# The last layer of a gated four-layer block on one core: a router moved into the attention, five shared blocks moved behind the routed tiles

## The reference, cut to what matters

```
x = x + tanh(g_xattn[3]) * attention(layernorm(x), ctx, ctx)     # 32 query heads of 8, 8 key/value heads
h = layernorm(x)
logits = h @ W_router.T                                          # 8 experts
probs  = softmax(logits);  weight, expert = top_k(probs, 2)
shared = (silu(h @ Wg) * (h @ Wu)) @ Ws_down                     # hidden width 704
shared = shared * sigmoid(h @ W_sgate.T)
sparse = sum over the two experts of weight * (silu(h @ We_g) * (h @ We_u)) @ We_down   # hidden width 176
x = x + tanh(g_ffn[3]) * (shared + sparse)
```

## Time and profile before

| | |
|---|---|
| median of 3 runs (lowest to highest) | 818.59 us (817.67 to 820.45) |
| span of the profiled execution | 816.7 us |
| PE, DVE, ACT, POOL busy | 707.3, 539.1, 353.9, 214.8 us |
| mean granted clock of PE | 0.945 |
| the fourth attention's last matmul ends | about 676 us |
| routed tiles on PE | 735.3 to 795.6 us |
| last work of DVE ends | 814.1 us |

### The profile page before, as it was taken

How to read it: one execution, slowest core, us unless ns; L and a number is a source line. 1 busy time by engine, 2 the same in 40 slices (tenths; PEclk the granted TensorE clock), 3 DMA queues, 4 the chain that set the end, 5 groups by cost and what they waited for, 6 DMA issues and landing times. The chain is left out here.

```text
span 816.7 us, 14003 instructions
## 1 busy us (share of the span) xinstructions
PE 707.3 (87%) x4479; PEld 467.5 (57%) x4485; DVE 539.1 (66%) x1627; ACT 353.9 (43%) x622; POOL 214.8 (26%) x307
## 2 busy tenths in 40 slices
PE   9999997988987785798868988986888899999995
PEld 4644466666764674576746767652233227776773
DVE  5786898788773879678861571657876756423554
ACT  2663455455445664221124314334488693212220
POOL 0002595002000132013313550632252220242340
PEclk9999999999998999789998999997599999999998
DMA  6994421040000310000160150011000043032315
GB/s 197 342 218 102 145 75 46 4 156 1 3 2 0 104 53 1 1 1 26 40 214 33 54 192 14 34 40 66 2 2 2 3 150 65 33 110 79 105 61 171
DMA packets 55566, 60.24 MB, mean 74 GB/s; under 512 B 13847, under 2 KB 48808, under 8 KB 55496
## 3 DMA queue, kind: packets, MB, share of 16 engines
q1 hardware_dynamic: 50408, 46.02, 19.6%
q0 software_dynamic: 4848, 13.28, 4.7%
q10 hardware_dynamic: 240, 0.05, 0.0%
HBM read 34.92 MB, written 24.20 MB: 72 GB/s over the span
## 5 line engine op out<-in xcount | busy, mean ns | idle before, releaser
L1928 ACT ACTIVATE arenas<-psum 128x512 f32<-128x512 f32 (+6 forms) x89 | 63.2, 732 | 60.3 <-PE psum L1134 51.6
L3156 DVE TENSOR_REDUCE arenas<-psum 128x2 f32<-128x512 f32 x96 | 62.0, 685 | 19.6 <-PE psum L1706 18.5
L943 POOL TENSOR_SCALAR arenas<-arenas,small 128x1024 f32<-128x1024 f32 x8 | 9.0, 1128 | 161.2 <-DVE small L2895 161.2
L960 POOL DMA_INDIRECT experts_l<-shared,small x30 | 29.1, 969 | 81.4 <-ACT shared L2228 72.8
L1123 PE MATMUL psum<-conb 128*128 128x512 bf16 x167 | 44.6, 413 | 4.9 <-ACT early L1928 3.1
L1134 PE MATMUL psum<-conb,shared 128*128 128x128 bf16 (+2 forms) x512 | 39.2, 231 | 10.3 <-issue 5.7
L1134 PE MATMUL psum<-con,early 128*128 128x128 f32 (+1 forms) x188 | 33.3, 287 | 15.5 <-ACT late L1928 4.4
L1134 PEld LDWEIGHTS psum<-conb,shared 128*128 128x128 bf16 (+2 forms) x512 | 34.0, 118 | 17.8 <-issue 14.9
L3121 DVE TENSOR_TENSOR shared<-shared,psum 128x128 f32<-128x128 f32 x30 | 8.6, 287 | 53.3 <-PE psum L1659 26.6
L1928 ACT ACTIVATE late<-psum 128x512 f32<-128x512 f32 (+1 forms) x51 | 25.6, 501 | 40.3 <-PE psum L1134 40.3
L2275 ACT ACTIVATE early<-psum 128x1024 f32<-128x1024 f32 x32 | 32.4, 1037 | 22.3 <-PE psum L1723 22.0
(11 more groups left out here) (436 smaller groups left out, 1792.2 us busy)
## 6 DMA issues: line engine op xcount, KB each, us to landing
sorted_l<-late SPq DMA_DIRECT2D x3, 1920.0 KB, 16.7
early<-sorted_l SPq DMA_DIRECT2D x6, 645.0 KB, 5.7
early<-in_L_ffn_sw SPq DMA_DIRECT2D x3, 1024.0 KB, 9.2
late<-sorted_l SPq DMA_DIRECT2D x23, 129.0 KB, 2.1
sorted_l<-late SPq DMA_DIRECT2D x1, 2944.0 KB, 23.5
early<-in_L_ffn_We_gate_up SPq DMA_DIRECT2D x2, 1408.0 KB
early<-in_L_ffn_expert_w SPq DMA_DIRECT2D x2, 1024.0 KB, 6.6
early<-in_L_ffn_w SPq DMA_DIRECT2D x1, 2048.0 KB, 8.2
```

Source lines behind the costliest of these rows:

```text
L960: pool.indirect_dma_start(expert_rows2[p], bass.IndirectOffsetOnAxis(dest2[p][:, i:i + 1], 0), out_r2[k], None).then_inc(outs_sent[k], 16)
L1928: act.activation(dst, view(v), ACT.Copy, scale=scale).then_inc(f.drained(i, key), 1)
L3156: dve.tensor_reduce(nm, q3d(f.slot(0, ("max", w, k)), 2, S), X, ALU.max, negate=True)\
```

## The change

The lines of the changed program are numbered by up to 29 more than those of the profile.
- The turns of batches 0 and 1 go into slot 59 of the attention, their logits into slot 62. DVE, not ACT, moves the turned rows. ACT takes the first pair's exponentials before it copies the last unit's result.
- Batch 2 is normalised alone between `results3(6)` and `results3(7)`, behind `gates3(0)`; batch 3 alone behind `results3(7)`. The turns of 2 and 3 and their logits stand between blocks of batch 0. The keys of banks 4 and 5 go in the order xT 2, gate 2, xT 3, gate 3.
- The rank stands behind the first block of batch 1.
- The half block of pair 1 stands before down product 1. The five full blocks of batch 3 follow the routed tiles: one each after steps 23 and 24 of the tile loop (its last step is 25), then two, down product 2, one, down product 3.
- DVE takes four of these blocks, adds batch 0's routed rows, adds down product 2, takes the fifth block, adds the routed rows of 1, 2 and 3, and down product 3 last.

```
@@ -648,14 +648,15 @@
...
-        plan("l3f", 0, A=([4, 5], 1, [(key, n) for p in range(2) for key in ("xT", "gate") for n in (2 * p, 2 * p + 1)]
-                          + [("dn", 0), ("dn", 1)]),
-             B=([0, 1, 2, 3], 1, [("sh", n, j) for n in range(B) for j in blocks3(n)]))
+        plan("l3f", 0, A=([4, 5], 1, [("xT", 0), ("xT", 1), ("gate", 0), ("gate", 1), ("xT", 2), ("gate", 2),
+                                      ("xT", 3), ("gate", 3), ("dn", 0), ("dn", 1)]),
+             B=([0, 1, 2, 3], 1, [("sh", n, j) for n in range(B - 1) for j in blocks3(n)] + [("sh", B - 1, SC3 - 1)]))
         plan("l3k", 0, A=([6], 1, [("rank",)]))
         tiles = range(TILES)
         plan("l3r", 0, X=([0, 1], 1, [("xT", i) for i in tiles]), U=([2, 3], 1, [("up", i) for i in tiles]),
              H=([4, 5], 1, [("hT", i) for i in tiles]), D=([6, 7], 1, [("dn", i) for i in tiles]))
-        plan("l3f", 1, A=([4, 5], 1, [("dn", 2), ("dn", 3)]))
+        BEHIND = range(SC3 - 1)
+        plan("l3f", 1, A=([4, 5], 1, [("dn", 2), ("dn", 3)]), B=([0, 1, 2, 3], 1, [("sh", B - 1, j) for j in BEHIND]))
...
+                routing = {59: [(row_turned3, 0), (row_turned3, 1)], 62: [(logits3, 0), (logits3, 1)]}
...
+                    for part, n in routing.get(g, ()):
+                        part(n)
...
-                last = ("sh", n | 1, SC3 - 1)
-                pe.wait_ge(fb.drained(0, last), fb.read(0, last))
+                last = ("sh", n | 1, BEHIND[-1] if n == B - 1 else SC3 - 1)
+                part = int(n == B - 1)
+                pe.wait_ge(fb.drained(part, last), fb.read(part, last))
...
+            def row_turned3(n):
+                p, s = n // 2, n % 2
+                pe.wait_ge(xn_ready["l3f"].sem, xn_ready["l3f"].count(n))
+                turn(pl["l3f"]["A"], 0, ("xT", n), [(P, c * S + t * P, rows3[p][:, s * T + t, c * P:(c + 1) * P])
+                                                    for c in range(DC) for t in range(T)], ident)
+
+            def logits3(n):
+                logits(pl["l3f"]["A"], 0, n, xnT3, r3T, E + 1)
+
+            def routed3(behind):
...
+                    if step >= TILES:
+                        next(behind, None)
...
-            banks_free("l3f", 0)
-            rows_turned3(0)
             tokens3(UNITS - 1)
-            for n in range(2):
-                logits(pl["l3f"]["A"], 0, n, xnT3, r3T, E + 1)
+            row_turned3(2)
             pe.wait_ge(ld["l3s"], 16 * 4)
-            shared3(0, blocks3(0))
-            rows_turned3(1)
-            for n in range(2, 4):
-                logits(pl["l3f"]["A"], 0, n, xnT3, r3T, E + 1)
-            shared3(1, blocks3(1))
+            shared3(0, 0, blocks3(0)[0:2])
+            logits3(2)
+            row_turned3(3)
+            shared3(0, 0, blocks3(0)[2:3])
+            logits3(3)
+            shared3(0, 0, blocks3(0)[3:])
+            shared3(0, 1, blocks3(1)[0:1])
             banks_free("l3k", 0)
             pe.wait_ge(picks_ready, TURNS)
             rank(pl["l3k"]["A"], 0, 2 * B, picked)
-            shared3(2, blocks3(2)[0:2])
+            shared3(0, 1, blocks3(1)[1:])
+            shared3(0, 2, blocks3(2)[0:2])
             shared_down3(0, 0)
-            shared3(2, blocks3(2)[2:])
+            shared3(0, 2, blocks3(2)[2:])
+            shared3(0, 3, [SC3 - 1])
             shared_down3(0, 1)
-            shared3(3, blocks3(3))
-            routed3()
-            banks_free("l3f", 1)
-            for n in range(2, 4):
-                shared_down3(1, n)
+
+            def behind_routed3():
+                for j in BEHIND[0:2]:
+                    shared3(1, 3, [j])
+                    yield
+                yield
+                shared3(1, 3, BEHIND[2:4])
+                shared_down3(1, 2)
+                shared3(1, 3, BEHIND[4:])
+                shared_down3(1, 3)
+
+            behind = behind_routed3()
+            routed3(behind)
+            alone(behind)
...
+                probabilities3(0)
                 sums3(UNITS - 1)
...
-            rows_moved3(0)
-            probabilities3(0)
-            shared3(0, 0)
-            rows_moved3(1)
+            row_moved3(2)
+            shared3(0, 0, blocks3(0)[0:2])
+            row_moved3(3)
+            shared3(0, 0, blocks3(0)[2:])
             probabilities3(1)
-            shared3(0, 1)
-            for n in range(2, 4):
-                shared3(0, n)
+            for n in range(1, 3):
+                shared3(0, n, blocks3(n))
+            shared3(0, 3, [SC3 - 1])
             routed3()
+            shared3(1, 3, BEHIND)
...
                 dve.wait_ge(x3_ready.sem, x3_ready.count(3))
                 norm_rows("l3f", 0, rows3[0])
                 reciprocals3(ON_POOL - 1)
+                f = pl["l3f"]["A"]
+                for n in range(2):
+                    dve.wait_ge(f.filled, f.full(0, ("xT", n)))
+                    dve.tensor_copy(xnT3[n], f.slot(0, ("xT", n))[:, 0:W]).then_inc(f.drained(0, ("xT", n)), 1)
                 results3(UNITS - 2)
+                gates3(0)
+                dve.wait_ge(x3_ready.sem, x3_ready.count(ON_POOL - 1))
+                alone(norm_steps("l3f", [2], [rows3[1][:, t, 0:D] for t in range(T)]))
                 results3(UNITS - 1)
+                alone(norm_steps("l3f", [3], [rows3[1][:, T + t, 0:D] for t in range(T)]))
...
-            gates3(0)
-            norm_rows("l3f", 1, rows3[1])
...
-            hidden3(0, 0, first_steps)
+            route3(0)
+            choices_of_pair(0)
+            hidden3(0, 0, blocks3(0)[0:1])
             gates3(1)
-            hidden3(0, 1, second_steps)
+            hidden3(0, 0, blocks3(0)[1:2])
+            route3(1)
+            choices_of_pair(1)
+            hidden3(0, 0, blocks3(0)[2:])
             alone(places(pl["l3k"]["A"], 0, places3, chosen, index_ready))
-            hidden3(0, 2, lambda j: add_shared(0, 0) if j == 1 else None)
+            hidden3(0, 1, blocks3(1))
+            hidden3(0, 2, blocks3(2)[0:2])
+            add_shared(0, 0)
+            hidden3(0, 2, blocks3(2)[2:])
+            hidden3(0, 3, [SC3 - 1])
             add_shared(0, 1)
-            hidden3(0, 3, lambda j: None)
             routed3()
-            add_shared(1, 2)
-            for n in range(B):
+            def added(n):
+                add_routed(n)
                 if n == B - 1:
                     add_shared(1, n)
-                add_routed(n)
                 dve.drain().then_inc(x_done.sem, 1)
+
+            hidden3(1, 3, BEHIND[0:4])
+            added(0)
+            add_shared(1, 2)
+            hidden3(1, 3, BEHIND[4:])
+            for n in range(1, B):
+                added(n)
```

More of the change, by code:

```diff
@@ L1807, in attention3, with shared3 @@
                         tokens3(w - 1)
+                    for part, n in routing.get(g, ()):
+                        part(n)
                 values3(UNITS - 1, 3)
-            def shared3(n, blocks):
+            def shared3(i, n, blocks):
                 f = pl["l3f"]["B"]
@@ L1813, in shared3 @@
                     if j < SC3 - 1:
-                        shared_up(f, 0, n, j, xnT3, P, j * P, H_S3 + j * P, ws_gu, ws_gu, 2 * H_S3)
+                        shared_up(f, i, n, j, xnT3, P, j * P, H_S3 + j * P, ws_gu, ws_gu, 2 * H_S3)
                         continue
-                    pe.wait_ge(f.drained(0, ("sh", n, j)), f.empty(0, ("sh", n, j)))
-                    v = f.slot(0, ("sh", n, j))
+                    pe.wait_ge(f.drained(i, ("sh", n, j)), f.empty(i, ("sh", n, j)))
+                    v = f.slot(i, ("sh", n, j))
                     for half in range(2):
@@ L1840, in shared_down3 @@
                 mm.then_inc(fa.filled, 1)
-            def rows_turned3(p):
-                for s in range(2):
-                    pe.wait_ge(xn_ready["l3f"].sem, xn_ready["l3f"].count(2 * p + s))
-                    turn(pl["l3f"]["A"], 0, ("xT", 2 * p + s), [(P, c * S + t * P, rows3[p][:, s * T + t, c * P:(c + 1) * P])
-                                                                for c in range(DC) for t in range(T)], ident)
-            def routed3():
+            def row_turned3(n):
[6 more added lines that the diff above has]
+            def routed3(behind):
                 fx, fu, fh, fd = (pl["l3r"][g] for g in "XUHD")
@@ L2283, in attention3, with row_moved3 @@
                             tokens_moved3(w - 1)
+                probabilities3(0)
                 sums3(UNITS - 1)
-            def rows_moved3(p):
-                for n in (2 * p, 2 * p + 1):
-                    move(pl["l3f"]["A"], 0, ("xT", n), xnT3[n], lambda v: v[:, 0:W])
+            def row_moved3(n):
+                move(pl["l3f"]["A"], 0, ("xT", n), xnT3[n], lambda v: v[:, 0:W])
             def probabilities3(p):
@@ L2296, in probabilities3, with shared3 @@
                 act.activation(c4_all, sgate[p][0], ACT.Exp, scale=-1.0).then_inc(sc3_ready.sem, 1)
-            def shared3(i, n):
+            def shared3(i, n, blocks):
```

(7 more changed lines are left out.)

10 lines of the change are left out of this document (removed).

## The result

The changed kernel takes **830.83 us** (827.45 to 832.84), against 819.31 us for the kernel before with its runs beside it: ratio 1.014, 95% interval 1.010 to 1.018. A second comparison on another chip gave 830.82 against 818.22, ratio 1.0144 (1.0112 to 1.0176). So it is slower, as forecast, but by 11.5 to 12.6 us and not by the 5.9 of the forecast. 830.8 lies outside the range of 819.5 to 827.5. The profiled execution has a span of 827.0 us and took 828.85.

What follows compares the result with a forecast made beforehand. PE sets the time up to the last tile; behind it the end hangs on the routed rows' return. The changed walk gives 821.3, clock 1.3 makes 822.6, and 1.9 from span to median 824.5 us; 8-in-10 range 819.5 to 827.5.

Steps and rivals of the forecast that it cites:

- attention ends later: Part 1: router turns and logits moved into the attention end it 2.5 us later, 678.6 instead of 676.1.
- small waits behind it: Between attention and batch 3's turn, PE waits 0.8 for ACT's copy, 0.6 for batch 2's rows, 0.7 for batch 3's.
- bank 5 at batch 3's logits: Batch 3's logits wait 2.8 us for bank 5 until DVE reads batch 2's logits at 691.5.
- the rank's wait, the bank behind it: PE waits 3.4 us at the rank for the choices, then 1.1 for bank 2, which DVE empties.
- first tile, less 5.9 of clock: End of PE's walk to the tiles: first routed tile at 736.2 against 735.3 before.
- first tile to the end of down product 3: Tile loop and moved blocks behind it: from the first tile at 736.2 to down product 3's end at 817.7.
- Part 4: Clock: rank waits cold, 1.3 us net; the 2.8 wait and the gap ahead of the tiles cancel; 821.3 becomes 822.6.
- the walk: PE's step-by-step path from attention to tiles and through the end, giving a first tile 0.9 later and span 821.3.
- all waits cold: Rival: half clock follows all new waits, adding 1.7 to 822.6: 824.3, time 826.2; chance 0.17.
- no bank wait and no cold gap: Rival: DVE's chain runs 2.7 us shorter, bank 5 free at 688.8: 816.8, time 818.7, no change; chance 0.15.
- the rank comes in time: Rival: both pairs' choices ready when PE arrives, 9.0 of 9.8 us of waits go: time 813.8; chance 0.08.
- The return of the rows: Rival: the routed rows' return ends last, first batch back at 808.1: 821.8, time 823.7; chance 0.05.

Runs made afterwards that it cites:

- PE kept busy: Changed kernel with its waits kept, PE multiplying unread constants during them; run twice: 1.0091 of the kernel before (825.27 us) and 1.0092 (824.29 us).
- the key order: Changed kernel with keys ordered xT 2, xT 3, gate 2, gate 3 and batch 3 turned ahead of batch 2's logits: 1.0083 of before, 825.89 us.
- the router behind the attention: Changed kernel with new key order and ACT's exponentials earlier, first pair's turns and logits back behind the attention: 1.0040 of before, 820.93 us.
- two edits of order: Changed kernel with both the new key order and ACT's second-pair exponentials moved earlier: 1.0035 of before, 820.52 us.
- ACT's order: Changed kernel with ACT taking the second pair's exponentials ahead of the tanh of batch 0's last two blocks: 1.0069 of before, 822.91 us.
- the waits filled: Changed kernel, both order edits, work moved into remaining waits: 0.9970 of before (815.96 us), again 0.9972 (815.48); gap ahead of tiles kept busy too, 0.9951 (815.00).
- the kernel before with the end alone: Kernel before with batch 3's five blocks behind the tiles and pair 1's half block ahead of down product 1, no router moved: 1.0027, 820.39 us.

## Why the prediction was right in its steps and wrong in its size

The forecast's steps, its execution moved by the 0.9 us where it is compared:

| step of the prediction | forecast | measured |
|---|---|---|
| attention ends later | 2.5 | 677.56 + 0.9 - 676.14 = 2.3 |
| small waits behind it | 0.8, 0.6, 0.7 | 0.70, 0.63, 0.66 |
| bank 5 at batch 3's logits | 2.8 | 2.89 |
| the rank's wait, the bank behind it | 3.4, 1.1 | 3.08, 1.39 |
| rank, less the 3.3 of clock ahead of it | 701.2 | 703.11 + 0.9 - 3.3 = 700.7 |
| first tile, less 5.9 of clock (PE kept busy) | 736.2 | 741.85 + 0.9 - 5.9 = 736.9 |
| first tile to the end of down product 3 | 81.5 | 81.5 |
| end of down product 3 to the end of the span | 3.6 | 827.0 - 823.3 = 3.7 |
| clock | 1.3 | 5.9 |

**The step that failed is Part 4, the clock.** The walk without it lands on the measured one within 0.7 us at each place. Part 4 took one price for a cold stretch from one row (3.5 us at half clock, 1.7 lost), took the rank's as partly swallowed (1.3), and let the wait of 2.8 and the gap ahead of the tiles cancel. Measured: both new waits were cold, each with 6.7 to 6.8 us at half clock, and the gap ahead of the tiles was cold as before, so that nothing cancelled. By the runs with PE kept busy this cost 5.9 us up to the first tile, with all waits in place. That is 5.9 - 1.3 = 4.6 of the profile's own miss, 827.0 + 0.9 - 822.6 = 5.3; the other 0.7 is the walk. The median lies 6.3 above the forecast, 1.0 more than the profile's miss; the four runs of it spread over 5.4 us.

Two errors lie in that step. The length came from a single stretch and had no upper end, so even the rival "all waits cold" (826.2) was too low by 4.6: it had 3.0 us for both waits together. And the first stretch does more than lose its own time: it delays the tanh on which ACT's exponentials wait, so the rank's wait is not shortened by PE being slow: it is 3.08 here and 3.1 with the clock held at 1.00. A wait for something else would have hidden the slow PE ahead of it; here PE's own result was what the wait was for. One sign that the prediction named for itself failed with the clock: the first tile was to be within 2 us of 735.3, and came at 741.85 + 0.9 = 742.8.

Of the rivals: "no bank wait and no cold gap" and "the rank comes in time" fell by the rows. The return of the rows did not bind: 1.10 is all that PE waited behind down product 2, and DVE's last addition starts (823.49) right as down product 3 ends (823.33). Two slips of the working changed nothing: the sorted rows were due at 701.2 + 26.7 + 0.9 = 728.8, not 729.2, and DVE's chain would have had to run 2.7 / 7 = 0.4 us faster a step, not half a microsecond.

The gap ahead of the first tile, 1.8 to 2.3 us, stands in twelve of the fourteen profiles (in the others it is filled, or is the wait of 6.16). It was cold in nine of them and warm in three: the key order, the first with PE kept busy, the one with the router behind the attention. The Trainium skill (TensorE: Matmul & The Clock Gate, section "HAM oscillation") counts only gaps past a certain length, by which this one would have been warm. Nine profiles disagree and three agree.

## What to carry to other kernels

Read every key order of shared banks, and every list of the engine that feeds a wait, as a chain of waits of PE: here two edits of order, neither adding nor removing work, were worth 9 of 12 us. Price a wait of PE of 1.5 to 3 us as its own length plus a stretch at half clock behind it, with a range of nothing to 3.4 us lost (once here 10.3 / 2 = 5.1) rather than one number, and see whether that stretch lies ahead of something that the next wait is for. Work moved behind the last stage pays only if that stage can then start earlier: it was worth 4 us where the stage's data lay ready, and nothing where they did not.

## What the runs showed of the hardware

The length of a stretch at half clock was no constant, and neither was whether it came. Behind the wait of 2.9 us at batch 3's logits it lasted 6.7, 6.7 and 6.8 us in three profiles of versions with that wait and 3.4 in a fourth (ACT's order). Behind the wait ahead of the first tile (1.8 to 2.3) it was 3.4 to 3.5 us in eight profiles, 6.7 in one (ACT's order) and absent in three. Three waits of 0.95 to 1.32 us close together had none behind them in any of the three profiles with the waits filled, while 3.4 us came in the kernel before with the end alone, where no wait over 0.34 stood in the 15 us ahead. With the router behind the attention, a wait of 2.23 us was followed by 10.3:

```profile
684.00:694.30 10.30, 10.30 (x35) 9.04 (x35) 5.85 (x41) 2.33 (x11) 0.00 (x0) 0.50 0.01 2
```

Here and behind the logits' wait PE was busy for the whole stretch (10.30 of 10.30, 6.70 of 6.70), so a busy PE did not end it at once. What sets the length stays open. Runs of one kernel on one chip spread over 5 us and more (the kernel before 814.80 to 824.38); cold stretches that come or stay away would do that, but so does work far ahead of the change, and no run separates the two. A change of 0.5% has to be read from medians of many runs, and its mechanism from the windows of more than one profile.
